# Graph network kernel, third layer: score transposes, score copies and softmax steps put later on three engines

## The reference

```python
gl = (x @ W_l).reshape(n, H, F_OUT)
gr = (x @ W_r).reshape(n, H, F_OUT)
s = jax.nn.leaky_relu(gl[src] + gr[dst], NEG_SLOPE)
e = jnp.einsum('ehf,hf->eh', s, att)
m = jax.ops.segment_max(e, dst, num_segments=n)
p = jnp.exp(e - m[dst])
denom = jax.ops.segment_sum(p, dst, num_segments=n)
alpha = p / (denom[dst] + 1e-16)
msg = alpha[:, :, None] * gl[src]
out = jax.ops.segment_sum(msg, dst, num_segments=n)
```

## Time and profile before

| what | value |
|---|---|
| median of 3 runs | 4813.23 us (4812.66 to 4814.01) |
| span of the profiled execution | 6172.5 us |
| PE, DVE, ACT, POOL busy in it | 1601.1, 2873.7, 1131.4, 3511.2 us |
| third layer's gather loop in it | 2983.3 to 4653.7 us |

### The profile page before, as it was taken

The page is one execution under the profiler, slowest core; times in us unless marked ns, Lnnn a source line. Parts: engine busy times, 40 slices in busy tenths (PEclk is TensorE's granted clock), DMA queues, the critical chain, the costliest instruction groups (busy, mean ns, idle before and its releaser), DMA issues.

```text
span 6172.5 us, 31606 instructions
## 1 busy us (share of the span) xinstructions
PE 1601.1 (26%) x6543; PEld 810.8 (13%) x6543; DVE 2873.7 (47%) x7569; ACT 1131.4 (18%) x3424; POOL 3511.2 (57%) x3636
## 2 busy tenths in 40 slices
PE   5531110000000000003376566656564500000002
PEld 1421110000000000001122222222221400000001
DVE  2344444124345455444255555555556632443435
ACT  1100000000000000001155555555555500000000
POOL 4356666756666666664634544454452576666764
PEclk7765555555555555556688888888887655555555
DMA  4211222221222222221123333333334221222222
GB/s 139 106 53 62 67 64 71 67 81 54 58 64 71 62 69 68 64 71 37 49 106 118 140 138 123 130 139 134 118 140 154 69 67 55 64 79 63 79 63 78
DMA packets 185944, 529.62 MB, mean 86 GB/s; under 512 B 70454, under 2 KB 75170, under 8 KB 169480
## 3 DMA queue, kind: packets, MB, share of 16 engines
q1 hardware_dynamic: 65816, 395.51, 16.9%
q0 software_dynamic: 117696, 129.81, 9.2%
q10 hardware_dynamic: 2224, 2.13, 0.1%
HBM read 185.57 MB, written 341.44 MB: 85 GB/s over the span
## 4 chain that ended last, share of the span: by engine, by line
DVE 39%; another core or an unknown queue 27%; issue 14%; PE 11%; ACT 6%; POOL 3%; DMA 0%; DVEq 0%; ACTq 0%; POOLq 0%
DVE AR L1672 11%; DVE AR L514 5%; DVE ps L779 5%; PE ps L1220 4%; POOL AR L190 2%; ACT AR L1371 2%; PE ps L1236 2%; DVE AR L850 2%; DVE AR L1385 2%; ACT AR L1227 1%; DVE AR L364 1%; DVE AR L1662 1%; PE ps L680 1%; DVE AR L803 1%
## 5 line engine op out<-in xcount | busy, mean ns | idle before, releaser
L190 POOL DMA_INDIRECT AR<-xt,Si x2496 | 2404.4, 963 | 1715.2 <-issue 744.3
L190 POOL DMA_INDIRECT AR<-y,R x752 | 711.3, 946 | 531.1 <-issue 228.7
L1385 DVE SCALAR_TENSOR_TENSOR AR<-AR,gf 128x390 f32<-128x390 f32 x780 | 484.2, 621 | 665.8 <-ACT AR L1371 469.9
L1220 PE MATMUL ps<-AR,WLR 128*128 128x512 f32 x1248 | 690.3, 680 | 152.2 <-ACT AR L1227 113.0
L1672 DVE SCALAR_TENSOR_TENSOR AR<-AR,gf 128x128 f32<-128x128 f32 x831 | 295.0, 355 | 470.8 <-DVE AR L1672 386.9
L1371 ACT ACTIVATE AR<-AR 128x64 f32<-128x64 f32 x1664 | 495.4, 346 | 0.0
L1227 ACT ACTIVATE AR<-ps 128x512 f32<-128x512 f32 x624 | 368.5, 591 | 231.3 <-remote 168.1
L779 DVE SCALAR_TENSOR_TENSOR ps<-ps,gf,AR 128x64 f32<-128x64 f32 x831 | 241.9, 291 | 288.2 <-remote 168.4
L514 DVE SCALAR_TENSOR_TENSOR AR<-AR,gf 128x64 f32<-128x64 f32 x831 | 237.2, 285 | 263.6 <-DVE AR L514 173.3
L190 POOL DMA_INDIRECT AR<-s,endi x196 | 215.7, 1101 | 179.5 <-issue 113.4
L1220 PEld LDWEIGHTS ps<-AR,WLR 128*128 128x128 f32 x1248 | 242.2, 218 | 462.2 <-issue 342.1
(11 more groups left out here) (326 smaller groups left out, 3045.4 us busy)
## 6 DMA issues: line engine op xcount, KB each, us to landing
s<-AR SPq DMA_DIRECT2D x51, 3168.0 KB
AR<-xd SPq DMA_DIRECT2D x104, 512.0 KB
s<-AR SPq DMA_DIRECT2D x51, 1024.0 KB
AR<-xt,Si POOLq DMA_INDIRECT x2496
s<-AR SPq DMA_DIRECT2D x53, 512.0 KB
s<-AR SPq DMA_DIRECT2D x51, 528.0 KB
xd<-AR SPq DMA_DIRECT2D x52, 512.0 KB
y<-AR SPq DMA_DIRECT2D x24, 1024.0 KB
```

The costliest lines, as they stand in the source:

```text
L190: g.indirect_dma_start(out=o, out_offset=None, in_=table, in_offset=bass.IndirectOffsetOnAxis(ap=idx, axis=0)).then_inc(S[sem], 16)
L1220: t.matmul(PS[2 + k % 3][:], WLR[:, ch * P:(ch + 1) * P], XT2[:, u % 6, :], start=True, stop=True).then_inc(S["pm"], 1)
L1385: m = v.scalar_tensor_tensor(out=Sv[:, j, 0:HW], in0=Sv[:, j - 1, 0:HW], scalar=gf[:, c * CH + j:c * CH + j + 1], in1=Sv[:, j, 0:HW], op0= ...
```

## The change

PE issues the four score transposes (`pf_t`) two groups later: not after the scores in group q = 1 but after the row transposes of group q = 3. ACT takes its first score copy (item 16) after item 9 and its second (item 17) after item 13, where both stood after item 7. DVE takes the six softmax steps after its steps 10 to 15, where they stood after steps 8 to 13. Nothing is added or taken out.

```diff
@@ chunk2_t
                 pt_t(e, u)
                 if u == 0:
                     continue
+                if c and q == 3:
+                    pf_t(e, c - 1)
                 for ch in range(3):
                     pm_t(e, u - 1, ch)
                     if c and q == 1:
                         pe_t(e, c - 1, ch)
                 if c and q == 1:
                     pe_t(e, c - 1, 3)
-                    pf_t(e, c - 1)
...
-        A_ORDER = (0, 1, 2, 3, 4, 5, 6, 7, 16, 17, 8, 9, 10, 11, 12, 13, 14, 15)
+        A_ORDER = (0, 1, 2, 3, 4, 5, 6, 7, 8, 9, 16, 10, 11, 12, 13, 17, 14, 15)
...
-                    if c + 1 < NCH and j >= CH - 8 and j - (CH - 8) < 6:
-                        soft2(e, c + 1, j - (CH - 8))
+                    if c + 1 < NCH and j >= CH - 6:
+                        soft2(e, c + 1, j - (CH - 6))
```

## The result

The changed kernel takes 4957.66 us, the median of 4 runs (4957.15 to 4958.48), against 4813.62 us before, also 4 runs. The ratio is 1.0298, with a 95% interval from 1.0286 to 1.0311: slower by 144 us. The forecast was 4960 us.

A forecast was written before the change was run, and what follows sets the result against it. The third layer's timed round was taken as 19.6 us without the profile's stall, at most 20.2 us if POOL holds it. A new round of 22.85 us over 50 rounds gave +147 us: 4960 us, range 4830 to 5000.

The forecast's parts named there:

- The two times: Profiled span 6172.5 us against timed median 4813.2 us; most of the difference read as belonging to the profiled execution.
- the stall: Third layer, profile before: ACT's copy waits long after PE's scores, 373.4 us lost in 47 rounds.
- the reading of 1.18 us a gather: Third layer at 1020 us leaves the three other gather loops 2849 us, so 1.18 us a gather in timed runs.
- The sentence on the profiled span: The profiled span may grow by less than the timed runs, since the stalls take up part of it.
- ACT and PE: Third-layer round: second score copy starts at 16.92 us after the exponential, ends 5.5 us later than before; ACT gains nothing.
- DVE: Waits for the second score copy; 5.65 us later the next exponential, at 22.85 us; ACT idle 3.6 us.
- The sum: Round longer by 3.23 us against 19.62, or 2.65 against 20.2; over 50 rounds +162 or +132, middle +147 us.
- against a round held by POOL at 20.2 us: If POOL's 16 gathers hold the old round at 20.2 us, the change adds 2.65 us a round, +132 us.
- the step from one round to fifty: One undisturbed round's loss taken for 50 full rounds of the third layer; the last two rounds left out.
- The stall is real: Rival: timed runs stall too, a loop through POOL holds the round; 0 to +160 us, middle 4885 us; chance 0.21.
- It is faster: Rival: PE's and ACT's waits at the score copies go, -55 to -90 us, 4740 us; chance 0.13.
- Only one half bites: Rival: moved softmax steps alone set the round, 21.6 us, +1.5 to +2.0 us each, 4888 to 4913 us; chance 0.12.

The follow-up runs named there:

- experiment 1: The kernel before, unchanged, profiled a second time; the single run took 4822.19 us.
- experiment 4: Kernel before with the late score transposes and copies, and DVE's six softmax steps all together after its step 12: 4831.47 us, ratio 1.0038.
- experiment 7: Changed kernel plus five matmuls of 384 columns a round, results unread, where PE sat idle: 4917.79 us, ratio 1.0201 to the kernel before.
- Experiments 3: Kernel before with only the score transposes and score copies late, softmax steps in their old place: 5000.13 us, ratio 1.0384.
- experiment 2: Kernel before with only the six softmax steps late, score transposes and copies in their old place: 4845.29 us, ratio 1.0064.
- experiment 8: Kernel before with late score transposes, score copies after items 9 and 11, softmax steps in their old place: 4879.65 us, ratio 1.0121.

## Why the prediction was right, and where it was lucky

**The two times.** The reading that the timed runs lack the stall was right, and the reading of 1.18 us a gather was near: experiment 1 shows 1.25 to 1.31 us, with the stall gone. But I called it a thing of profiling; it was a thing of that one profiled execution, since none of the ten later profiles has it, that of the same kernel included. What made it is open. The Trainium skill's rule in "NOTIFIC — the notification-queue block", section "7.1 Overflow: three behaviours, one of which stalls the engine", that the block writing the records holds its producers back, would explain the first profile; no run here shows that it did. The sentence on the profiled span, that it might grow by less than the timed runs, fell with it.

**ACT and PE.** Right to 0.2 us in the first round: copy at 17.08 us (16.92). It is at 17.10 us in experiment 4's rounds of 20.22 us, and 17.11 us in experiment 7, where the clock holds. ACT gained nothing, as worked out.

**DVE.** Right: the chain from copy to exponential is 3043.44 - 3037.66 - 0.25 = 5.53 us (5.65), DVE was 1.05 us early (1.2), and ACT's wait is 3.36 us (3.6). Experiments 3 and 4 show both parts, the copy's place and the sums in between, to be needed for the loss.

**The sum.** 147 us was forecast and 144 measured, but two of its terms were mis-sized, against each other, and it is luck that they nearly cancel. The forecast set 22.85 us against the middle of 19.62 and 20.2 us. The step "against a round held by POOL at 20.2 us" had the gathers too cheap: 20.96 us, so that only 22.85 - 20.96 = 1.89 us a round would be lost, 95 us and not 147. And the step from one round to fifty took the undisturbed round as it stood: I had given ACT an idle time of 3.6 us before the exponential, behind which PE stands as well, for 4.16 us in the trace, and not asked what follows from that. No term of the sum stood for the clock. The fall of the clock costs 1.04 us a round, 52 us over 50 rounds. Experiment 7 gives 47 of them back. 95 + 52 = 147 us; the means of the 50 rounds in the two traces, 23.89 and 21.08 us, make 141 us.

**Rivals.** "The stall is real" is refuted by experiment 1. "It is faster": PE's wait for the first copy did go, but nothing of it reached the end, as ACT left no place for it. The Trainium skill, page "Perfetto Trace Analysis", section "Optimization Strategies", says that when TensorE is idle one should optimize the engines that are "blocking the critical path". The prediction had left out that condition, and it is what decides here: PE's wait of 0.71 us was not on the chain that ends the round. It went, nothing was gained, and one of 4.16 us came. "Only one half bites" had the right place and the wrong price: experiment 2 is that half, a round of 21.2 us with the clock up (21.6), +30 us and not +75 to +100, since POOL's 20.96 us were the mark to be passed, and the larger part of the 30 us lies in the rounds with the low clock.

## What to carry to other kernels

When a producer is put later in one engine's order, its place sets when the last consumer starts, and everything that is queued between the consumer's own steps counts with it. Work off that chain from the undisturbed round, compare with what holds the round now, and only what exceeds that is lost. Then ask what each new idle time on PE does to the clock.

When a profiled span and the timed median are far apart, profile again before making a sum of it.

## What the runs showed of the hardware that was not expected

- After 4.16 us of idle time on PE the granted clock falls to 1.2 GHz for some 3.4 us of nearly every full round, 0.6 us after PE has work again. In experiment 7, where matmuls for nothing leave 0.94 us of that time idle, it stays at 2.4 GHz. In between, PE waits 2.84 us at this place in experiment 8 and the clock falls in every second round; 2.52 us in experiment 2, and it falls in every third.
- POOL's gathers take longer in the third layer, where the DMA engines move 195 GB/s against 79 and 78 GB/s in its neighbours (experiment 1): 1.005 us against 0.95 us, and in the changed kernel 865.47 / 833 = 1.04 us. The cause is not shown.
